# First score pass of an attention and mixture-of-experts block: two heads at a time in the two halves of the array

## The chip, the cores and the metric

The kernel runs on one core of one Trainium2 chip. Its time is the time on the device in microseconds, the median of several executions. Before the change three executions took 592.57 us in the median, 589.27 us at the least and 598.64 us at the most.

## The reference

The input is eight images ("image" here is one entry of the batch) of 512 tokens with 128 channels, in float32. For each of them

```python
h = _layernorm(x, axis=-1) * (1 + ca) + sa
x = x + ga * _L0_attn_ref(h, ...)
h = _layernorm(x, axis=-1) * (1 + cb) + sb
x = x + gb * _L0_ffn_ref(h, ...)
```

The six modulation rows (`sa`, `ca`, ...) come from a small product of a condition with `wmod`. The attention has 16 heads of 8 channels, is causal, and ends in a projection and a layer norm:

```python
att = jnp.einsum('bhtd,bhsd->bhts', q, k) * (1.0 / math.sqrt(Dh))
att = jnp.where(causal[None, None], att, -jnp.inf)
att = jax.nn.softmax(att, axis=-1)
o = jnp.einsum('bhts,bhsd->bhtd', att, v)
```

The feed-forward part has one shared expert of width 128 and eight routed experts of width 64, of which a token's two likeliest count; all eight are computed and multiplied by a coefficient that is zero for the others:

```python
shared_out = jnp.einsum('bsd,dh->bsh', shared_act * shared_up_out, shared_down)
expert_out = jnp.einsum('etd,edh->eth', jax.nn.silu(gate) * up, experts_down)
routed = jnp.einsum('eth,te->th', expert_out, coef)
```

## The kernel before

**Scores.** q and k are split into three bf16 parts each (`q_parts`, `k_parts`), written to DRAM and read back as stacks: for each head 72 rows (`KROWS`) hold all nine combinations of a part of q with a part of k, so that one bf16 product over 72 rows gives nearly exact scores. Scores are computed twice. The **first pass** (`s1`, L1003 to L1019) serves the row maximum alone: queries on the 128 partitions, `w` keys along the columns (128, 256, 384 or 512, by the block `qt` of queries), then a second product that adds the causal mask to the last 128 columns (L1017). VectorE reduces each bank to `row_max` (L844). A bank takes one head of 512 or 384 columns, two of 256, or four of 128, so a group of four heads takes 11 units (`S1_UNITS`); two banks alternate, and unit u waits until unit u - 2 is reduced. The maxima are split into three bf16 parts by two small VectorE operations (`msplit`, L853 and L855), transposed by TensorE (`max`, L1051), copied by ScalarE, and put by a DMA on the SP queue into three further rows of the stack of q. The **second pass** (`s2`, L1030) computes the scores transposed over 75 rows, with the maximum subtracted. ScalarE takes the exponential (L650), GpSimd cuts the triangle (L558), and `pv` (L1044) multiplies by the values, four heads at a time in four groups of 32 array columns.

**Banks.** There are eight PSUM banks: two for `s1`, two for `s2`, `pv_bank`, `misc`, `gate_bank`, `up_bank`. `misc` is shared by all small products in turn (`MISC_TASKS`): each waits until the one before it is read. The gate product (L1097) goes to `gate_bank` and the up product (L1108) to `up_bank`; VectorE multiplies the two (L922, L927). `up_bank` also holds the projection `y` (L1065, L1068), which ScalarE scales into `y_sb` (L683) and VectorE multiplies by gamma (L873).

**Order.** Each engine works through its queue in order. The order is written out by hand as tables: an image is four stages (`s` 0 to 3, one for each group of four heads) of 30 steps. `S1_STEPS`, `S2_STEPS` and `PV_STEPS` place the score and value units, `EXTRA` all other tasks. In stage s the first pass works on group s, the second on group s - 1, the values on s - 1 and s - 2. `LATER` shifts single tasks on VectorE, GpSimd or ScalarE by some steps. The feed-forward part of an image runs in the stages of the next one; the last image's runs alone at the end (`LAST`). `PROLOGUE` is what comes ahead of the first image.

**Queues.** The SP queue issues, in order, the writes of q and k parts (L438 to L443), the loads of the stacks (`load_stacks`, six a group, L422), and the DMA of the maxima (L456).

## Time and profile before

| what | value |
|---|---|
| median of 3 executions | 592.57 us (589.27 to 598.64) |
| profiled execution, its own time | 592.91 us |
| its span, first to last instruction | 591.2 us |
| mean granted TensorE clock | 0.916 |
| TensorE busy | 520.3 us, 88% |
| VectorE busy | 416.9 us, 71% |
| ScalarE busy | 299.3 us, 51% |
| GpSimd busy | 244.5 us, 41% |

The busy time of TensorE counts a matmul to its modelled end, and matmuls overlap, so the distance between two starts tells more of what one costs than its duration. Idle time of an engine counts only where another one waits for it. The granted clock is the share of the full 2.4 GHz that TensorE was given; it has two levels here, 1.0 and 0.5.

### The profile page before, as it was taken

What the parts mean: (1) busy time and instruction counts of PE and PEld (TensorE: products, weight loads), DVE (VectorE), ACT (ScalarE), POOL (GpSimd) and SP (SyncE); (2) the same over time, 40 slices, a digit from 0 to 9 for tenths busy, and PEclk for the clock granted to TensorE, in tenths of its full rate; (3) what the DMA queues carried; (4) which work ended last, traced back from release to release, by engine and by line L of the source; (5) the groups of instructions that cost most, each with busy time, mean ns of one, the idle gap of its engine ahead of it and who ended that gap; (6) DMA issues with size and microseconds to landing.
All of it is one profiled execution on the core that took longest, in us unless ns stands there. A gap on an engine that the chain in (4) does not pass through costs nothing.

```text
span 591.2 us, 10213 instructions
## 1 busy us (share of the span) xinstructions
PE 520.3 (88%) x3628; PEld 281.4 (48%) x3643; DVE 416.9 (71%) x877; ACT 299.3 (51%) x614; POOL 244.5 (41%) x299
## 2 busy tenths in 40 slices
PE   1647989899989999899989998999989998999567
PEld 1513434455644464456455554546445643645234
DVE  7458988687776868776878777686767677573045
ACT  1104546656565546655565647454655646455320
POOL 6024335713662257524572366235742424034210
PEclk9957899899997999899989999899979998599769
DMA  5171412321324113321332132412331121001000
GB/s 139 48 191 51 148 46 83 107 74 42 77 59 149 42 51 87 112 54 45 84 103 81 42 78 59 149 42 60 77 131 24 37 82 38 0 2 37 0 1 18
DMA packets 46930, 40.65 MB, mean 69 GB/s; under 512 B 8088, under 2 KB 42656, under 8 KB 46880
## 3 DMA queue, kind: packets, MB, share of 16 engines
q1 hardware_dynamic: 39232, 36.92, 22.1%
q10 hardware_dynamic: 7648, 3.09, 2.0%
q8 instruction: 29, 0.48, 0.4%
q14 instruction: 21, 0.17, 0.1%
HBM read 24.91 MB, written 14.68 MB: 67 GB/s over the span
## 4 chain that ended last, share of the span: by engine, by line
PE 72%; DVE 13%; ACT 6%; issue 4%; DMA 2%; SPq 1%; POOL 0%; DVEq 0%; POOLq 0%; ACTq 0%
PE pv_bank L1044 13%; PE s_bank L1015 11%; PE s_bank L1030 10%; DVE row_max L844 7%; PE gate_bank L1097 6%; PE gate_bank L1130 6%; PE up_bank L1108 6%; PE misc L973 5%; PE s_bank L1017 4%; PE misc L995 3%; ACT probs L650 3%; PE misc L1000 2%; PE up_bank L1068 2%; PE misc L1078 2%; ACT square L676 2%
## 5 line engine op out<-in xcount | busy, mean ns | idle before, releaser
L844 DVE TENSOR_REDUCE row_max<-s_bank 128x1 f32<-128x512 f32 (+3 forms) x352 | 213.0, 637 | 82.1 <-PE s_bank L1017 79.5
L650 ACT ACTIVATE probs<-s_bank 128x512 f32<-128x512 f32 x320 | 183.4, 598 | 105.9 <-PE s_bank L1030 103.4
L1015 PE MATMUL s_bank<-k_stack,q_stack 72*128 72x256 bf16 (+3 forms) x512 | 142.4, 319 | 17.2 <-DMA k_stack<-k_scr 8.3
L558 POOL TENSOR_SCALAR_AFFINE_SELECT probs<-probs 128x512 f32<-128x512 f32 (+1 forms) x96 | 80.2, 841 | 120.5 <-ACT probs L650 120.4
L1030 PE MATMUL s_bank<-q_stack,k_stack 75*128 75x128 bf16 (+3 forms) x512 | 118.7, 310 | 3.8 <-ACT probs L650 1.7
L1017 PE MATMUL s_bank<-causal,ident_bf 128*128 128x128 bf16 x512 | 103.8, 228 | 0.0
L1044 PE MATMUL pv_bank<-probs,v_aug 128*32 128x512 f32 (+3 forms) x1024 | 97.3, 485 | 0.0
L1015 PEld LDWEIGHTS s_bank<-k_stack,q_stack 72*128 72x128 bf16 x512 | 51.0, 100 | 81.1 <-DVE row_max L844 49.7
L1030 PEld LDWEIGHTS s_bank<-q_stack,k_stack 75*128 75x128 bf16 x512 | 42.0, 100 | 48.2 <-ACT probs L650 17.5
L1017 PEld LDWEIGHTS s_bank<-causal,ident_bf 128*128 128x128 bf16 x512 | 52.3, 102 | 24.3 <-issue 16.6
L543 POOL TENSOR_TENSOR hidden<-hidden,coef_sb 128x512 f32<-128x512 f32 x28 | 35.6, 1271 | 43.2 <-ACT coef_sb L696 43.0
L1097 PE MATMUL gate_bank<-h2T,wg 128*128 128x512 f32 x76 | 42.7, 644 | 0.1
L1108 PE MATMUL up_bank<-h2T,wu 128*128 128x512 f32 x76 | 41.1, 622 | 0.0
L1130 PE MATMUL gate_bank<-wd_b,hidden 128*128 128x128 f32 x280 | 37.2, 280 | 0.4
L1044 PEld LDWEIGHTS pv_bank<-probs,v_aug 128*32 128x32 f32 x1024 | 24.4, 114 | 27.5 <-issue 22.7
L1130 PEld LDWEIGHTS gate_bank<-wd_b,hidden 128*128 128x128 f32 x280 | 33.9, 191 | 2.4 <-issue 1.6
L864 DVE RECIPROCAL denom<-misc 128x16 f32<-128x16 f32 x32 | 8.1, 253 | 35.6 <-PE misc L973 35.6
L659 ACT ACTIVATE u_sb<-pv_bank 128x512 f32<-128x512 f32 x32 | 19.1, 597 | 25.1 <-PE pv_bank L1044 25.1
L922 DVE SCALAR_TENSOR_TENSOR silu_sb<-tanh_sb,gate_bank 128x512 f32<-128x512 f32 x38 | 25.9, 683 | 4.9 <-ACT tanh_sb L701 4.3
L701 ACT ACTIVATE tanh_sb<-gate_bank 128x512 f32<-128x512 f32 x38 | 22.7, 596 | 11.6 <-PE gate_bank L1097 11.6
L927 DVE SCALAR_TENSOR_TENSOR hidden<-silu_sb,up_bank 128x512 f32<-128x512 f32 x38 | 25.9, 680 | 3.4 <-PE up_bank L1108 3.4
L578 POOL TENSOR_SCALAR coef_parts<-coef 128x32 bf16<-128x32 f32 x8 | 2.4, 300 | 58.2 <-DVE coef L916 58.2
(150 smaller groups left out, 625.2 us busy)
## 6 DMA issues: line engine op xcount, KB each, us to landing
q_stack<-q_scr SPq DMA_DIRECT2D x96, 96.0 KB
k_stack<-k_scr SPq DMA_DIRECT2D x96, 96.0 KB
k_scr<-k_parts SPq DMA_DIRECT2D x14, 256.0 KB, 3.2
q_scr<-q_parts SPq DMA_DIRECT2D x7, 384.0 KB, 2.3
k_scr<-k_parts SPq DMA_DIRECT2D x7, 384.0 KB, 3.0
x_res<-in_L_attn_x SPq DMA_DIRECT2D x8, 256.0 KB, 3.4
out_x<-out_sb SPq DMA_DIRECT2D x8, 256.0 KB, 2.6
x_in<-in_L_attn_x ACTq DMA_DIRECT2D x7, 256.0 KB, 2.9
```

The costliest lines, as they stand in the source:

```text
L543: nc.gpsimd.tensor_tensor(hidden[:, a, :], hidden[:, a, :], coef_sb[:, :], ALU.mult).then_inc(weighted, 1)
L558: nc.gpsimd.affine_select(out=view, in_=view, compare_op=ALU.is_ge, fill=0.0, base=0, pattern=pat, channel_multiplier=-1).then_inc(probs_r ...
L650: nc.scalar.activation(dst, src, ACT.Exp, scale=SCALE).then_inc(exp_done, 1)
L844: nc.vector.reduce_max(row_max[s % 2][:, 0, h:h + nh, qt], s1_bank[u % 2][:, 0:nh * w].rearrange("p (h k) -> p h k", h=nh), AX_X).then_inc ...
L973: final = nc.tensor.transpose(dst[:, P * t:P * (t + 1)], src(t), idn[:, :])
L1015: nc.tensor.matmul(dst[:, w * i:w * (i + 1)], q_stack[0:KROWS, h, P * qt:P * (qt + 1)], k_stack[0:KROWS, h, 0:w], start=True, stop=False)
L1017: final = nc.tensor.matmul(dst[:, w * (i + 1) - P:w * (i + 1)], ident_bf[:, :], causal[:, :], start=False, stop=True)
L1030: final = nc.tensor.matmul(dst[:, at:at + w], k_stack[0:MROWS, hh, P * j:P * (j + 1)], q_stack[0:MROWS, hh, P * j:T], start=True, stop=True)
L1044: final = nc.tensor.matmul(pv_bank[VC * h:VC * (h + 1), P * j:T], v_aug[(it - (n < 0)) % 2][:, j, GH * g + h, :], probs[g % 2][:, h, P_AT[ ...
L1097: nc.tensor.matmul(gate_of(it, a)[:, :], wg[:, P * a:P * (a + 1)], h2T[:, :], start=True, stop=True).then_inc(gate_written, 1)
L1108: nc.tensor.matmul(up_of(it, a)[:, :], wu[:, P * a:P * (a + 1)], h2T[:, :], start=True, stop=True).then_inc(up_written, 1)
L1130: last_mm = nc.tensor.matmul(down_of(it)[:, P * t:P * (t + 1)], hidden[:, m, P * t:P * (t + 1)], wd_b[:, m, :], start=False, stop=(a == MB ...
```

## The change

The first pass takes two heads at a time. The first 64 of the 72 rows of a head are used. The even head's rows lie on partitions 0 to 63 (`q_stack`, `k_stack` as before), the odd head's on partitions 64 to 127 of two new tiles (`q_odd`, `k_odd`). The two products are built with a tile size of 64 by 128 at row 0 and at row 64, and write to two different banks. Their mask products follow, over all 128 rows. `S1_PAIRS` has six entries for a group, each of which fills two banks, so a group has 12 units. Three banks turn round; the third was `up_bank`. The up products of all images but the last one's go through `misc`, and `y` into `gate_bank`, where it is scaled and multiplied by gamma in place. `msplit` moves from VectorE to GpSimd. The stacks take 12 loads a group in place of six, and k is written in five parts. In the prologue x is loaded first, the copy `cond_rep` (`spread`) and the gate products come later. All tables of the order are new.

```diff
-S1_UNITS = ([(h, 1, 3) for h in range(GH)] + [(h, 1, 2) for h in range(GH)]
-            + [(0, 2, 1), (2, 2, 1)] + [(0, 4, 0)])
+S1_PAIRS = [((0,), 3), ((2,), 3), ((0,), 2), ((2,), 2), ((0, 2), 1), ((0, 2), 0)]
...
-S1_STEPS = [[0, 0, 7, 10, 12, 13, 14, 16, 16, 17, 21],
+S1_STEPS = [[0, 7, 12, 13, 14, 19],
...
-    "xin", "xs", "cond", "xn", "late", "xt", "gates0", "q", "gates1", "k", "gates2", "stack", "v", "gates3")]
+    "xin", "xs", "cond", "xn", "late", "xt", "q", "spread", "k", "stack", "v", "gates0", "gates1", "gates2", "gates3")]
...
+def hidden_made(eng, it, a, up_read, misc_read):
+    if it == B:
+        eng.wait_ge(up_read, a + 1)
+    elif it > 0:
+        eng.wait_ge(misc_read, misc_at(it, (s_of(it, "u", a), "u", a)) + 1)
...
-        s1_bank = [bank("s1_bank0"), bank("s1_bank1")]
+        s1_bank = [bank(f"s1_bank{i}") for i in range(3)]
...
-        Q_DMAS = 2 * PARTS
-        SCR_DMAS = 1 + 1 + 2 * (PARTS - 1)
+        Q_DMAS = 4 * PARTS
+        SCR_DMAS = PARTS + K_SLOTS
...
         def up_of(it, a):
-            return s1_bank[1] if last(it) and a % 2 else up_bank
+            return s1_bank[1 + a % 2] if last(it) else misc
...
+                for i, r in enumerate(ROTATIONS):
...
+                    for stack, odd, scr, at in ((q_stack, q_odd, q_scr, 0), (k_stack, k_odd, k_scr, DH * r)):
+                        sp.dma_start(stack[rows, heads, :],
+                                     scr[heads, at:at + SROWS, :].rearrange("h r t -> r h t")).then_inc(stacked[g], 16)
+                        sp.dma_start(odd[odd_rows, pair, :],
+                                     scr[GH * g + 1:GH * g + GH:2, at:at + DH * odd_parts, :]
+                                     .rearrange("h r t -> r h t")).then_inc(stacked[g], 16)
...
+                if name == "msplit":
+                    z = row_max[s % 2][:, :, :, :].rearrange("p k h t -> p k (h t)")
+                    n2 = it * (G * 2) + 2 * s
+                    pool.wait_ge(s1_reduced, it * (G * U1) + U1 * (s + 1))
+                    nc.gpsimd.tensor_tensor(z[:, 1, :], z[:, 0, :], upper(z[:, 0, :]), ALU.subtract).then_inc(max_step, 1)
+                    pool.wait_ge(max_step, n2 + 1)
+                    nc.gpsimd.tensor_tensor(z[:, 2, :], z[:, 1, :], upper(z[:, 1, :]), ALU.subtract).then_inc(max_step, 1)
...
+                    for odd in range(2):
+                        u = U1 * s + 2 * a + odd
+                        h = heads[0] + odd
+                        dve.wait_ge(s1_written, it * (G * U1) + (u + 1))
+                        nc.vector.reduce_max(row_max[s % 2][:, 0, h:h + 2 * nh - 1:2, qt],
+                                             s1_bank[u % 3][:, 0:nh * w].rearrange("p (h k) -> p h k", h=nh),
+                                             AX_X).then_inc(s1_reduced, 1)
...
                     need(pe, s1_reduced, it * (G * U1) + (u - 1))
                     w = P * (qt + 1)
-                    dst = s1_bank[u % 2]
-                    for i in range(nh):
-                        h = GH * s + h0 + i
-                        nc.tensor.matmul(dst[:, w * i:w * (i + 1)], q_stack[0:KROWS, h, P * qt:P * (qt + 1)],
-                                         k_stack[0:KROWS, h, 0:w], start=True, stop=False)
-                        final = nc.tensor.matmul(dst[:, w * (i + 1) - P:w * (i + 1)], ident_bf[:, :], causal[:, :],
-                                                start=False, stop=True)
-                    final.then_inc(s1_written, 1)
+                    even, odd = s1_bank[u % 3], s1_bank[(u + 1) % 3]
+                    for i, h in enumerate(heads):
...
+                        nc.tensor.matmul(even[:, cols], q_stack[0:HALF, hh, queries], k_stack[0:HALF, hh, 0:w],
+                                         start=True, stop=False)
+                        nc.tensor.matmul(odd[:, cols], q_odd[HALF:P, hh // 2, queries], k_odd[HALF:P, hh // 2, 0:w],
+                                         start=True, stop=False)
+                        for dst in (even, odd):
+                            final = nc.tensor.matmul(dst[:, w * (i + 1) - P:w * (i + 1)], ident_bf[:, :], causal[:, :],
+                                                    start=False, stop=True)
+                            if i == len(heads) - 1:
+                                final.then_inc(s1_written, 1)
...
                 if name == "u":
-                    if a == 0:
-                        pe.wait_ge(y_scaled, it)
                     if not last(it):
-                        need(pe, up_read, it * MB + (a - MB))
+                        take_misc(it, (s, "u", a))
```

**TensorE, stage 1 of a steady image**, up to the transpose of the maxima (`max`). Before:

```order
L1015 MATMUL s_bank<-k_stack,q_stack 128x128
L1017 MATMUL s_bank<-causal,ident_bf 128x128
L1030 MATMUL s_bank<-q_stack,k_stack 128x128
L1030 MATMUL s_bank<-q_stack,k_stack 128x384
L1030 MATMUL s_bank<-q_stack,k_stack 128x256 x2
L1051 MATMUL misc<-ident_bf,row_max 48x128
L1030 MATMUL s_bank<-q_stack,k_stack 128x256 x2
L1044 MATMUL pv_bank<-probs,v_aug 32x512 x4
L1000 MATMUL misc<-wv,h1T 128x128 x4
```

With the change (L1051 is the even head's product, L1053 the odd's, L1056 the mask, L1070 the second pass, L1084 the values, L1091 the transpose):

```order
L1051 MATMUL s_bank<-k_stack,q_stack 128x128
L1053 MATMUL s_bank<-k_odd,q_odd 128x128
L1056 MATMUL s_bank<-causal,ident_bf 128x128 x2
L1070 MATMUL s_bank<-q_stack,k_stack 128x128
L1070 MATMUL s_bank<-q_stack,k_stack 128x384
L1070 MATMUL s_bank<-q_stack,k_stack 128x256 x4
L1084 MATMUL pv_bank<-probs,v_aug 32x512 x4
L1091 MATMUL misc<-ident_bf,row_max 48x128
L1051 MATMUL s_bank<-k_stack,q_stack 128x512
```

Two products of the second pass and the value product have moved to the front of the transpose, and the two heads' products stand side by side.

**TensorE, stage 2**, where the products of the feed-forward part stand (L1137 is a gate product, L1146 an up product, L1007 a transpose). With the change:

```order
L1146 MATMUL misc<-h2T,wu 128x512
L1137 MATMUL gate_bank<-h2T,wg 128x512
L1007 MATMUL misc<-ident,u_sb 128x128 x4
L1070 MATMUL s_bank<-q_stack,k_stack 128x128
L1070 MATMUL s_bank<-q_stack,k_stack 128x384
...
L1070 MATMUL s_bank<-q_stack,k_stack 128x256 x4
L1146 MATMUL misc<-h2T,wu 128x512
L1137 MATMUL gate_bank<-h2T,wg 128x512
L1007 MATMUL misc<-ident_bf,coef_parts 128x128 x4
L1084 MATMUL pv_bank<-probs,v_aug 32x512 x4
```

Before, the same products stand so:

```order
L973 MATMUL misc<-ident,u_sb 128x128 x4
L1030 MATMUL s_bank<-q_stack,k_stack 128x256 x2
L1108 MATMUL up_bank<-h2T,wu 128x512
...
L1044 MATMUL pv_bank<-probs,v_aug 32x512 x4
L1097 MATMUL gate_bank<-h2T,wg 128x512
L973 MATMUL misc<-ident_bf,coef_parts 128x128 x4
L1108 MATMUL up_bank<-h2T,wu 128x512
L1051 MATMUL misc<-ident_bf,row_max 48x128
```

The up products now write `misc`, as the transposes around them do, and each of these waits until the one before it is read.

**The SP queue, first image**, between the first loads and the maxima. Before there are six loads like these for a group; with the change a group has twelve:

```order
L422 DMA k_stack<-k_scr 24x4x512
L438 DMA q_scr<-q_parts 96x1536
L440 DMA k_scr<-k_parts 96x1536
L442 DMA k_scr<-k_parts 96x1024
L443 DMA k_scr<-k_parts 96x512
L442 DMA k_scr<-k_parts 96x512
L443 DMA k_scr<-k_parts 96x1024
L422 DMA q_stack<-q_scr 24x4x512
L422 DMA k_stack<-k_scr 24x4x512
```

```order
L439 DMA k_odd<-k_scr 16x2x512
L459 DMA q_scr<-q_parts 12x8x512 x3
L462 DMA k_scr<-k_parts 12x8x512 x5
L437 DMA q_stack<-q_scr 24x4x512
L439 DMA q_odd<-q_scr 24x2x512
L437 DMA k_stack<-k_scr 24x4x512
L439 DMA k_odd<-k_scr 24x2x512
L437 DMA q_stack<-q_scr 24x4x512
L439 DMA q_odd<-q_scr 24x2x512
```

The writes of q and k have become eight (three and five), and loads of `q_odd` and `k_odd` stand between those of the stacks.

## Rows read from the trace of the kernel before

**Rows 1.** The page, parts 1 and 4: busy time by engine, and the chain.

```profile
PE 520.3 (88%) x3628; PEld 281.4 (48%) x3643; DVE 416.9 (71%) x877; ACT 299.3 (51%) x614; POOL 244.5 (41%) x299
...
PE 72%; DVE 13%; ACT 6%; issue 4%; DMA 2%; SPq 1%; POOL 0%; DVEq 0%; POOLq 0%; ACTq 0%
```

**Rows 2.** Span and mean granted TensorE clock.

```profile
core 0: 591.2 us, clock 0.916
```

**Rows 3.** Groups by shape, PE: count, busy us, mean ns, idle before by releaser.

```profile
L1015 PE MATMUL s_bank<-k_stack,q_stack 72*128 72x512 bf16 x128 | 50.9, 425 | 10.7 <-DMA k_stack<-k_scr 8.3 <-DVE row_max L844 2.1
...
L1051 PE MATMUL misc<-ident_bf,row_max 128*48 128x128 bf16 x32 | 7.5, 233 | 15.2 <-issue 13.2 <-ACT h1T L623 1.0 <-DVE row_max L855 0.9
```

**Rows 4.** Waits: who for whom, us in total, times, longest.

```profile
PEld s_bank L1015 <- DVE row_max L844: 49.7, 133, 3.0
```

**Rows 5.** Timeline, PE, first-pass products of 512 columns: start us, us.

```profile
250.08 0.38 PE L1015 MATMUL s_bank<-k_stack,q_stack 72*128 72x512 bf16 x1
250.30 0.22 PE L1017 MATMUL s_bank<-causal,ident_bf 128*128 128x128 bf16 x1
```

**Rows 6.** Timeline, products of 128 columns, then the value products.

```profile
258.91 0.22 PE L1015 MATMUL s_bank<-k_stack,q_stack 72*128 72x128 bf16 x1
258.92 0.10 PEld L1017 LDWEIGHTS s_bank<-causal,ident_bf 128*128 128x128 bf16 x1
258.97 0.22 PE L1017 MATMUL s_bank<-causal,ident_bf 128*128 128x128 bf16 x1
...
259.21 0.22 PE L1017 MATMUL s_bank<-causal,ident_bf 128*128 128x128 bf16 x1
...
259.36 0.64 PE L1044 MATMUL pv_bank<-probs,v_aug 128*32 128x512 f32 x4
```

**Rows 7.** Timeline, PE, 256 columns, and the product with one row.

```profile
272.14 0.27 PE L1015 MATMUL s_bank<-k_stack,q_stack 72*128 72x256 bf16 x1
272.25 0.22 PE L1017 MATMUL s_bank<-causal,ident_bf 128*128 128x128 bf16 x1
...
272.79 0.38 PE L1124 MATMUL gate_bank<-zero_row 1*128 1x512 bf16 x1
273.11 0.38 PE L1130 MATMUL gate_bank<-wd_b,hidden 128*128 128x128 f32 x1
```

**Rows 8.** Timeline before the transpose of the maxima in stage 1.

```profile
240.49 0.39 PE L1030 MATMUL s_bank<-q_stack,k_stack 75*128 75x256 bf16 x2
...
240.91 1.26 POOL L571 TENSOR_TENSOR x_res<-x_res,beta_a 128x512 f32<-128x512 f32 x1
241.02 1.18 DVE L855 TENSOR_TENSOR row_max<-row_max 128x16 f32<-128x16 f32 x1
...
242.30 0.27 PE L1051 MATMUL misc<-ident_bf,row_max 128*48 128x128 bf16 x1 [1.42 <-issue]
```

**Rows 9.** Windows: length, busy of five engines, clock, DMA share, GB/s.

```profile
218.00:281.10 63.10, 60.29 (x450) 32.75 (x450) 48.30 (x104) 37.38 (x77) 30.82 (x36) 0.97 0.27 77
344.50:409.10 64.60, 61.79 (x450) 33.45 (x450) 48.30 (x104) 37.38 (x77) 30.82 (x36) 0.95 0.26 75
242.20:245.60 3.40, 3.30 (x14) 1.14 (x15) 3.23 (x9) 1.28 (x3) 2.13 (x2) 0.50 0.29 109
34.40:88.00 53.60, 43.36 (x278) 20.04 (x279) 46.77 (x87) 21.81 (x40) 20.59 (x20) 0.78 0.35 99
```

**Rows 10.** Groups by shape, DVE.

```profile
L927 DVE SCALAR_TENSOR_TENSOR hidden<-silu_sb,up_bank 128x512 f32<-128x512 f32 x38 | 25.9, 680 | 3.4 <-PE up_bank L1108 3.4
```

**Rows 11.** Groups by shape, POOL.

```profile
L580 POOL TENSOR_TENSOR coef_rest<-coef,coef_parts 128x32 f32<-128x32 f32 x8 | 2.0, 245 | 0.7
```

**Rows 12.** Timeline of the first image, SP queue and first product.

```profile
31.41 0.35 SPq L438 DMA_DIRECT2D q_scr<-q_parts  x1
...
34.38 0.59 PE L1015 MATMUL s_bank<-k_stack,q_stack 72*128 72x512 bf16 x1 [8.30 <-DMA k_stack<-k_scr]
...
37.35 0.31 SPq L422 DMA_DIRECT2D q_stack<-q_scr  x1
```

180 lines of the change are left out of this document (95 added, 85 removed), and 27 rows, old and new, of tables (LATER, S1_STEPS, S2_STEPS).

## The prediction, made before the changed kernel was run

> **What bounds the kernel now.** I first read the busy times and the chain of the page [rows 1]: TensorE is busy 88% of the span and has 72% of the chain, VectorE 71% and 13%. So TensorE's stream of products is the bound in most of the span, and the question is what else stands in it. The granted clock is 0.916 in the mean [rows 2]. The windows [rows 9] say where the rest lies. In two steady images TensorE is busy 60.29 of 63.10 us and 61.79 of 64.60 us with the same 450 products. In the first image it is busy only 43.36 of 53.60 us, beside a VectorE that is busy 46.77 us: there VectorE's reductions bound, and TensorE has 10 us to spare.
>
> The groups and waits [rows 3, 4] show what TensorE waits for: 15.2 us ahead of the 32 transposes of the maxima, and 2.1 us on VectorE ahead of the widest first-pass products. Their weight loads waited 49.7 us, 133 times, but weights are loaded ahead, so this is mostly no loss of products. The timeline [rows 8] shows the worst wait ahead of a transpose: its products end near 240.9, VectorE's second `msplit` operation takes 1.18 us beside a GpSimd operation of 1.26 us, and the transpose starts at 242.30 after 1.42 us of idle time. The clock then is 0.50 for the next 3.40 us [rows 9]. The two steady images differ in length by 1.5 us, with clocks of 0.97 and 0.95.
>
> **The change, step by step.** Distances between starts at full clock are 0.22 us for 512 columns, 0.11 for 256 and 0.06 for 128 [rows 5 to 7]; 384 lies between, 0.17.
>
> *Columns saved.* A pair streams once where two heads streamed one after the other. That is 0.22 + 0.17 + 0.11 + 0.06 = 0.56 us for each of 64 pairs of heads, 35.8 us at full clock, 39.1 at the mean of 0.916. That the two do run side by side is not in this trace for row halves. The nearest row is the value product: four products in four column groups last 0.64 us together [rows 6]. I take full overlap, less 0.01 us a pair (256 pairs, 2.6 us). The bounds are that and no saving at all.
>
> *Pauses between modes.* The two products use the array in another mode than the mask products behind them. Where the trace changes mode it shows a pause. From a mask product to the value product it is 259.36 - 259.21 = 0.15 us in place of 0.06 [rows 6]; out of the product with one row, 512 columns take 273.11 - 272.79 = 0.32 us in place of 0.22 [rows 5, 7]. So 0.09 to 0.10 us a change, 0.095 taken. Neighbours that differ in mode number 238 in the order before and 746 in the new one: 508 more, 48.3 us. No row shows a change between modes that both use all 128 columns and at least 64 rows, so the lower bound is nothing, the upper 48.3 us.
>
> The Trainium skill ("TensorEngine Tiling (Array Packing)", Key Properties) says that any change of the tiling mode, not of the tile, drains TensorE; by it the full 48.3 us stand, without it the kernel would be 48.3 us faster than my sum.
>
> *Net stream:* 48.3 + 2.6 - 39.1 = +11.8 us, +12. In the first image 64 of the changes (6 us) fall into TensorE's spare 10 us [rows 9]: -5.
>
> *Weight loads.* They last 0.10 us (258.92), yet the products stand 0.06 us apart [rows 6], all on the same rows of the array. So loads are hidden already and the halves hide nothing more: 0. The Trainium skill ("TensorE: Matmul & The Clock Gate", Part 3, The mechanism) says that a load overlaps a running product only if their row groups differ. The trace here disagrees: by the rule 256 odd heads' loads of 0.10 us, 25.6 us, would go too; by the row nothing.
>
> *`msplit` on GpSimd.* It leaves VectorE, and with it the collision of [rows 8]. GpSimd's nearest operation, of twice the width, takes 245 ns [rows 11]; two take 0.5 us. What queues behind them on GpSimd is the selection of the next triangle, which the value product needs only a stage later. The cover has grown as well: in stage 1 two more second-pass products (0.22 us) and a value product (about 0.5 us) stand ahead of the transpose. I take 60% of the 15.2 us [rows 3]: -9. Bounds 0 and -15.
>
> *Third bank.* A pair waits for the first half of the pair before, so TensorE may run one and a half units ahead instead of one. The visible waits are small: -3.5 in the steady images, bounds 0 and -8. The cost of 32 more reductions lies on VectorE, which loses `msplit` and is not the bound in steady images: 0.
>
> *Clock.* In each of six images a stretch at half clock stands behind the wait of [rows 8]. It costs 1.5 us per 3.4 us, by the two images of [rows 9] (clock 0.97 against 0.95). Four images have a clock of 0.95 like the second (about 6.8 us, 3.0 us lost), two 0.97 (1.5 lost): 15 us to be had if the wait is gone. But the pauses leave TensorE without products more often elsewhere. I take -10, bounds -15 and +11.
>
> *Up products through `misc`.* 35 of the 40 now hold it until VectorE has multiplied, 680 ns [rows 10] behind a busy queue. In stage 2 the transposes of `u_sb` are queued behind one up and one gate product, about 1.7 us of cover; VectorE has to go through the routing's small operations first. Behind this transpose stand the second-pass products and all of ScalarE's exponentials. I take 1 us an image, +7; bounds 0 and 35 x 0.68 = 24. `y` in the gate bank: the first gate product comes a stage later, 0.
>
> *SP queue and prologue.* Six writes and their landing took from 31.41 to 37.35, 5.9 us; now eight, +2 us ahead of the second group. A DMA takes the queue 0.31 to 0.35 us at the least to issue [rows 12], so six more loads are +2 us ahead of the first products, which started at 34.38, less about 1 for a k that is ready earlier. The second group's loads and the maxima behind them are late too. +3, bounds -2 and +8. Later stages have over 30 us between load and use: 0.
>
> **Sum.** Profiled execution 592.9 + 12 - 5 - 9 - 3.5 - 10 + 7 + 3 = 587.4, so 587 us. The profiled execution is 0.3 us above the median of 592.6, so no correction. A change of under 2% (580.7 to 604.4) can't be told from none.
>
> **Rivals.**
>
> *All waits and half-clock stretches gone.* The pauses don't bring the clock down, and the hand-offs through `misc` are covered: 587 - 5 - 7 = 575. For it: the collision is gone for certain, and the order now places work ahead of the transpose. Against: VectorE still has four halves of first-pass work in a row before the end of stage 1.
>
> *No pause in the new mode.* 587 - 48 + 5 = 544. For it: no row shows this mode. Against: both kinds of change that rows do show pause alike.
>
> *Slower: the clock.* Pauses of 0.19 us a pair are densest where the 128 and 256 columns stand: a pair of 128 columns has 0.18 us of products and 0.19 of pause. With the waits around, such a place may do what 1.42 us of idle did. The old stretches stay (+10), and each of seven images gets another of 3.4 us (7 x 1.5 = +10.5): 608. It decides from about twelve stretches of 3.4 us on beyond those of the forecast (17.4 us to the bound of 604.4, 1.5 each). For it: TensorE's pauses grow from 23 to 71 us. Against: each pause is a tenth of a microsecond, and the wait of [rows 8] is fourteen times as long.
>
> *The pair doesn't overlap,* so the change doesn't do what it says: the odd product waits for the even one. 587 + 39 = 626. Against: the column groups overlap.
>
> **Chances.** Forecast 0.42 (its own range 580 to 598), everything gone 0.24, no pause 0.08, the clock 0.18, no overlap 0.05, the rest (a late queue, a longer hold of `misc`, 600 to 615) 0.03. The range of 8 in 10 takes in the forecast, the 575 with 8 us below it and the 608 with 2 above it: 567 to 610. It leaves out 544 and 626. Faster by over 2%: 0.24 + 0.08 + 0.02 of the forecast's lower end = 0.34. Slower: 0.18 + 0.05 + 0.02 = 0.25. Within: 0.41.
>
> **What would show it.** Starts of even and odd products 0.01 us apart prove the overlap, 0.2 us refute it. From the start of a 512-column pair to its mask product 0.31 us show the pause, 0.22 us refute it. Idle time ahead of the transposes should fall to about 6 us, that ahead of TensorE's transposes of `u_sb` grow by up to 7. A steady image should have a clock of 0.97 or more and last 63 to 64 us; 66 us with 0.93 would be the slower rival. The first product of the first pass should start at 35 to 37 us. My forecast is wrong above all if the clock goes either way, since that one term can weigh 25 us.

## The result: 2.2% slower

The changed kernel takes 605.48 us (median of 4 runs, 604.77 to 606.85) against 593.93 (4 runs, 589.27 to 598.64) of the kernel before: a ratio of 1.0224, interval [1.0155, 1.0293]. So it is slower beyond the interval, though not for certain by over 2%. Ratios here and below are of the fast executions alone and medians of all, and the kernel before has slow ones as well (up to 8 in 19, 594 to 599 us at a lower clock), so a ratio can stand some tenths of a per cent above that of the medians. The profiled execution took 605.75 us. The forecast was 587 with a range of 567 to 610, so the time lies inside the range and on the other side of no change.

The page's parts 1 and 4 and the clock, which answer to [rows 1, 2]:

```profile
PE 520.3 (86%) x3628; PEld 251.1 (42%) x3643; DVE 379.7 (63%) x845; ACT 295.4 (49%) x614; POOL 256.0 (42%) x363
...
PE 75%; DVE 10%; ACT 5%; SPq 3%; DMA 3%; issue 2%; ACTq 1%; POOL 1%; POOLq 0%; DVEq 0%
...
core 0: 604.0 us, clock 0.938
```

TensorE is as long busy as before, although 256 products no longer stream by themselves. VectorE lost 37 us of work and 3% of the chain. The clock is better than before, and the kernel is slower all the same.

Windows (length, busy of five engines, clock, DMA share, GB/s) of before, first the six images between the first and the last. Then of the changed kernel: its first image, the six, and one of them. The other windows of before are in [rows 9].

```profile
88.00:473.90 385.90, 368.26 (x2690) 200.37 (x2701) 289.76 (x625) 224.21 (x462) 183.26 (x216) 0.96 0.26 75
```

```profile
36.10:99.50 63.40, 48.99 (x280) 18.67 (x280) 43.23 (x83) 21.30 (x40) 22.95 (x28) 0.63 0.33 98
99.50:489.80 390.30, 365.94 (x2691) 176.61 (x2702) 261.10 (x601) 221.35 (x462) 191.13 (x263) 1.00 0.28 82
230.50:295.30 64.80, 60.75 (x450) 29.40 (x452) 43.51 (x100) 36.89 (x77) 32.12 (x44) 1.00 0.28 83
```

Of the 12.8 us between the spans, 1.7 lie ahead of the first product (36.1 against 34.4), 9.8 in the first image (63.4 against 53.6, clock 0.63 against 0.78) and 4.4 in the six images, where the clock is now 1.00 but for the first (66.1 us at 0.98). The last image and the tail gave 3 back.

Groups by shape on TensorE, answering to [rows 3]:

```profile
L1070 PE MATMUL s_bank<-q_stack,k_stack 75*128 75x512 bf16 x128 | 48.5, 395 | 7.7 <-DMA q_stack<-max_rows 3.9 <-ACT probs L677 3.8
L1051 PE MATMUL s_bank<-k_stack,q_stack 64*128 64x512 bf16 x64 | 26.2, 409 | 8.1 <-DMA k_odd<-k_scr 6.3 <-DVE row_max L876 1.7
L1051 PE MATMUL s_bank<-k_stack,q_stack 64*128 64x384 bf16 x64 | 22.1, 346 | 6.6 <-DVE row_max L876 6.6
L1051 PE MATMUL s_bank<-k_stack,q_stack 64*128 64x256 bf16 x64 | 18.4, 288 | 6.1 <-DVE row_max L876 6.0
L1051 PE MATMUL s_bank<-k_stack,q_stack 64*128 64x128 bf16 x64 | 14.8, 232 | 3.7 <-DVE row_max L876 3.7
L1070 PE MATMUL s_bank<-q_stack,k_stack 75*128 75x256 bf16 x128 | 23.4, 286 | 4.4 <-ACT probs L677 3.8
L1146 PE MATMUL misc<-h2T,wu 128*128 128x512 f32 x70 | 37.2, 612 | 3.4 <-DVE logit L913 3.4
L1091 PE MATMUL misc<-ident_bf,row_max 128*48 128x128 bf16 x32 | 7.4, 232 | 2.9 <-issue 1.5 <-POOL row_max L586 1.3
```

The same groups of before that aren't in [rows 3] (first pass of 384, 256 and 128 columns, second pass of 512 and 256, up products):

```profile
L1015 PE MATMUL s_bank<-k_stack,q_stack 72*128 72x384 bf16 x128 | 43.8, 343 | 4.9 <-DVE row_max L844 4.3
L1015 PE MATMUL s_bank<-k_stack,q_stack 72*128 72x256 bf16 x128 | 29.3, 281 | 0.1
L1015 PE MATMUL s_bank<-k_stack,q_stack 72*128 72x128 bf16 x128 | 19.1, 226 | 1.6 <-DVE row_max L844 1.4
L1030 PE MATMUL s_bank<-q_stack,k_stack 75*128 75x512 bf16 x128 | 45.9, 391 | 2.0 <-ACT probs L650 1.2 <-DMA q_stack<-max_rows 0.8
L1030 PE MATMUL s_bank<-q_stack,k_stack 75*128 75x256 bf16 x128 | 26.2, 293 | 0.8 <-ACT probs L650 0.2
L1108 PE MATMUL up_bank<-h2T,wu 128*128 128x512 f32 x76 | 41.1, 622 | 0.0
```

The 12.3 us that went from ahead of the transposes (15.2 to 2.9) are back elsewhere, in the first image and in the six. First-pass products of 384 to 128 columns wait 16.4 us (before 6.6), second-pass products of 512 and 256 columns 12.1 (before 2.8), up products 3.4 (before 0). In the six images alone TensorE's idle time, the length of the window less the busy time, grew from 17.6 to 24.4 us.

Timelines of the changed kernel (start us, us): a pair of 128 columns, then one of 384, each with its mask products.

```profile
253.82 0.23 PE L1051 MATMUL s_bank<-k_stack,q_stack 64*128 64x128 bf16 x1
253.82 0.23 PE L1053 MATMUL s_bank<-k_odd,q_odd 64*128 64x128 bf16 x1
...
253.98 0.29 PE L1056 MATMUL s_bank<-causal,ident_bf 128*128 128x128 bf16 x2
```

```profile
247.12 0.33 PE L1051 MATMUL s_bank<-k_stack,q_stack 64*128 64x384 bf16 x1
247.13 0.33 PE L1053 MATMUL s_bank<-k_odd,q_odd 64*128 64x384 bf16 x1
247.39 0.29 PE L1056 MATMUL s_bank<-causal,ident_bf 128*128 128x128 bf16 x2
```

The two heads start 0.01 us apart or less: they run side by side. From the pair to its first mask product it is 0.16 us at 128 columns, in place of 0.06, and 0.27 at 384, in place of 0.17. So the pause on leaving this mode is 0.10 us at either width, as between the modes of [rows 5 to 7]. A pair of 128 columns saves 0.06 us and pays two pauses. Counted over the whole trace, neighbours that differ in mode are 746 (before 238), as the forecast had counted them.

### The profile page after: what moved, and what is told of

The parts are those of the page before. It is cut to its first block, busy times and chain, and to the rows that moved or that the text cites. A ratio compares the mean times of both kernels' runs of the same rounds, so it can differ in the third digit from the quotient of the medians.

```text
span 604.0 us, 10440 instructions
## 1 busy us (share of the span) xinstructions
PE 520.3 (86%) x3628; PEld 251.1 (42%) x3643; DVE 379.7 (63%) x845; ACT 295.4 (49%) x614; POOL 256.0 (42%) x363
## 4 chain that ended last, share of the span: by engine, by line
PE 75%; DVE 10%; ACT 5%; SPq 3%; DMA 3%; issue 2%; ACTq 1%; POOL 1%; POOLq 0%; DVEq 0%
PE pv_bank L1084 14%; PE s_bank L1070 10%; PE s_bank L1051 10%; PE s_bank L1056 8%; PE gate_bank L1137 6%; PE gate_bank L1168 6%; PE misc L1146 5%; DVE row_max L876 5%; PE misc L1007 5%; PE misc L1029 3%; ACT probs L677 3%; PE gate_bank L1108 2%; PE misc L1034 1%; DVE x_n L827 1%; PE misc L1091 1%
## 5 line engine op out<-in xcount | busy, mean ns | idle before, releaser
L876 DVE TENSOR_REDUCE row_max<-s_bank 128x1 f32<-128x384 f32 (+3 forms) x384 | 212.5, 595 | 89.0 <-PE s_bank L1056 86.8
L677 ACT ACTIVATE probs<-s_bank 128x512 f32<-128x512 f32 x320 | 181.5, 594 | 139.4 <-PE s_bank L1070 136.8
L1070 PE MATMUL s_bank<-q_stack,k_stack 75*128 75x128 bf16 (+3 forms) x512 | 116.8, 310 | 13.5 <-ACT probs L677 8.7
L577 POOL TENSOR_SCALAR_AFFINE_SELECT probs<-probs 128x512 f32<-128x512 f32 (+1 forms) x96 | 76.8, 800 | 110.3 <-ACT probs L677 110.2
L1051 PE MATMUL s_bank<-k_stack,q_stack 64*128 64x512 bf16 (+3 forms) x256 | 81.6, 319 | 24.5 <-DVE row_max L876 18.1
L1084 PE MATMUL pv_bank<-probs,v_aug 128*32 128x512 f32 (+3 forms) x1024 | 96.4, 465 | 0.3 <-POOL probs L577 0.3
L1053 PE MATMUL s_bank<-k_odd,q_odd 64*128 64x512 bf16 (+3 forms) x256 | 81.6, 319 | 0.0
L1056 PE MATMUL s_bank<-causal,ident_bf 128*128 128x128 bf16 x512 | 75.5, 231 | 0.0
L1070 PEld LDWEIGHTS s_bank<-q_stack,k_stack 75*128 75x128 bf16 x512 | 43.5, 101 | 60.0 <-ACT probs L677 33.6
L1051 PEld LDWEIGHTS s_bank<-k_stack,q_stack 64*128 64x128 bf16 x256 | 23.8, 93 | 86.9 <-DVE row_max L876 49.9
L1056 PEld LDWEIGHTS s_bank<-causal,ident_bf 128*128 128x128 bf16 x512 | 29.5, 98 | 40.5 <-issue 28.9
L1137 PE MATMUL gate_bank<-h2T,wg 128*128 128x512 f32 x76 | 41.0, 621 | 1.1 <-issue 1.1
L1146 PE MATMUL misc<-h2T,wu 128*128 128x512 f32 x70 | 37.2, 612 | 3.4 <-DVE logit L913 3.4
L1084 PEld LDWEIGHTS pv_bank<-probs,v_aug 128*32 128x32 f32 x1024 | 22.8, 111 | 34.0 <-issue 27.4
L953 DVE SCALAR_TENSOR_TENSOR silu_sb<-tanh_sb,gate_bank 128x512 f32<-128x512 f32 x38 | 26.1, 686 | 14.1 <-ACT tanh_sb L727 14.1
L727 ACT ACTIVATE tanh_sb<-gate_bank 128x512 f32<-128x512 f32 x38 | 22.7, 596 | 22.4 <-PE gate_bank L1137 22.4
L961 DVE SCALAR_TENSOR_TENSOR hidden<-silu_sb,misc 128x512 f32<-128x512 f32 x35 | 24.1, 688 | 14.7 <-PE misc L1146 12.7
```

The source lines that it names most:

```text
L577: nc.gpsimd.affine_select(out=view, in_=view, compare_op=ALU.is_ge, fill=0.0, base=0, pattern=pat, channel_multiplier=-1).then_inc(probs_r ...
L677: nc.scalar.activation(dst, src, ACT.Exp, scale=SCALE).then_inc(exp_done, 1)
L876: nc.vector.reduce_max(row_max[s % 2][:, 0, h:h + 2 * nh - 1:2, qt], s1_bank[u % 3][:, 0:nh * w].rearrange("p (h k) -> p h k", h=nh), AX_X ...
L1051: nc.tensor.matmul(even[:, cols], q_stack[0:HALF, hh, queries], k_stack[0:HALF, hh, 0:w], start=True, stop=False)
L1053: nc.tensor.matmul(odd[:, cols], q_odd[HALF:P, hh // 2, queries], k_odd[HALF:P, hh // 2, 0:w], start=True, stop=False)
L1056: final = nc.tensor.matmul(dst[:, w * (i + 1) - P:w * (i + 1)], ident_bf[:, :], causal[:, :], start=False, stop=True)
```

## The experiments

The forecast's sum had five places where it could fail: pairs, queue, third bank, shared bank, and the gain from waits and clock. The first runs take the change apart; the later ones build on the kernel before. Ratios are to runs of before on the same chip (medians 593.3 to 593.8, where not given otherwise). A difference between two runs by their ratios can come out some us apart from that of their medians; where it matters both are given.

### The pauses: masks behind both pairs

```diff
-                                         start=True, stop=False)
+                                         start=(i == 0), stop=False)
...
+                    for i, h in enumerate(heads):
...
-                                                    start=False, stop=True)
+                                                    start=False, stop=(i == len(heads) - 1))
```

> The changed kernel, but in units with two pairs of heads (256 and 128 columns) all four products of the 64-row mode come first and the four mask products after them. That is two changes of mode fewer in each of 64 units, 128 fewer. Theory A (each change of mode costs TensorE 0.095 to 0.10 us, and in steady images nothing hides it): 12 to 13 us less than the changed kernel's 605.5, so 593 us, and less only by what falls into waits in the first image, 591 to 597. Rival B (the pauses lie in TensorE's waits for VectorE, and the loss comes from the new waits and hand-offs): within 2 us of 605.5.

Measured: 593.85 us, ratio 1.0073 [1.0040, 1.0105]. A hit: 11.6 us for 128 changes of mode (two in each of the 64 units that hold two pairs, those of 256 and 128 columns). Its first image and its six:

```profile
36.50:98.20 61.70, 44.77 (x278) 17.27 (x278) 43.61 (x83) 21.28 (x40) 22.64 (x28) 0.70 0.34 99
98.20:479.20 381.00, 358.35 (x2703) 171.98 (x2702) 261.01 (x601) 220.83 (x462) 190.75 (x264) 1.00 0.29 84
```

The six images took 9.3 us less than in the change at the same clock. The six images hold 96 of the 128 changes, so the pauses are on the path in steady images, and at 0.10 us each they weigh what the forecast gave them.

### No pairs, and no second queue entries

```diff
-  nc.tensor.matmul(even[:, cols], q_stack[0:HALF, hh, queries], k_stack[0:HALF, hh, 0:w],
+  nc.tensor.matmul(even[:, cols], q_stack[0:KROWS, hh, queries], k_stack[0:KROWS, hh, 0:w],
...
-  nc.tensor.matmul(odd[:, cols], q_odd[HALF:P, hh // 2, queries], k_odd[HALF:P, hh // 2, 0:w],
+  nc.tensor.matmul(odd[:, cols], q_stack[0:KROWS, hh + 1, queries], k_stack[0:KROWS, hh + 1, 0:w],
```

> The changed kernel with its order, banks and loads, but both products of a pair are taken over 72 rows of the full stacks, so they run one after the other in the mode of the mask products. 512 changes of mode are gone, and the columns are streamed twice. Theory A: -49 us of pauses, +36 to +39 us of columns, so 592 to 596 us. Rival C (the pairing pays and something else lost the time): 605.5 + 36 us or nearly, 630 to 642. Both heads' products should start 0.22 us apart at 512 columns in place of 0.01.

Measured: 595.95 us, 1.0116 [1.0033, 1.0199]. A hit. The pairs cost 9.5 us net in this kernel (6.4 by the ratios). Not 512 changes of mode went, as the expectation says: counted in the trace, neighbours that differ in mode are 273 in place of 746, so 473 went. Some pairs stand beside a product of yet another mode, where a pause stays without them. The other 35 above the 238 of before belong to the new order.

The second run takes out the loads of `k_odd` and `q_odd` as well (the `sp.dma_start(odd[...])` of the change; four entries of the queue per pair of parts become two).

> As e2, and the loads of the odd heads' stacks, which nothing reads now, are left out: six loads a group. Theory D (the longer SP queue costs time in the first image alone): the first product starts 2 us earlier, TensorE's 3.1 us wait for the maxima's DMA goes, and the kernel is 3 to 6 us faster than e2. Rival: the queue is hidden by other waits of the first image, within 1.5 us of e2.

Measured: 593.63 us, 1.0024 [0.9985, 1.0062]; 2.3 us for the queue by the medians (5.4 by the ratios), so between the 3 to 6 of theory D and the 1.5 of its rival. TensorE's wait for the DMA of the maxima went as expected (2.9 to 0.9 us ahead of the second pass), but the first product starts 1.0 us earlier, not 2. Windows of the two, first image and six:

```profile
36.20:99.40 63.20, 50.06 (x278) 24.07 (x279) 43.24 (x83) 21.30 (x40) 22.97 (x28) 0.64 0.33 97
99.40:483.60 384.20, 361.84 (x2702) 194.27 (x2700) 260.91 (x601) 220.65 (x462) 190.84 (x263) 1.00 0.29 83
```

```profile
35.20:95.20 60.00, 46.54 (x279) 22.36 (x280) 43.62 (x83) 21.29 (x40) 22.14 (x28) 0.70 0.31 78
95.20:478.30 383.10, 360.69 (x2703) 194.03 (x2701) 260.90 (x601) 220.65 (x462) 191.68 (x264) 1.00 0.26 67
```

The first image without pairs is 63.2 us, with pairs 63.4: the pauses and the saved columns together make no difference there. The six images are 384.2 against 390.3, 1.0 us an image. The queue shows at the start (first product 35.2 against 36.2) and in the first image (60.0 against 63.2).

### Pairs only where they are wide

```diff
+                        if qt == 3:
...
+                        else:
+                            for dst, j in ((even, hh), (odd, hh + 1)):
+                                nc.tensor.matmul(dst[:, cols], q_stack[0:KROWS, j, queries], k_stack[0:KROWS, j, 0:w],
+                                                 start=True, stop=False)
```

> The changed kernel, with pairs in the 64-row mode only where they have 512 columns; the narrower ones are taken over 72 rows one after the other, as in e2. Against the changed kernel 384 changes of mode go (-38 us) and 0.67 us of columns a group come back (+21 us). Theory A: 605.5 - 17 = 588.5, or from e2 596 - 1.3 = 594.7, so 588 to 595 us, and under e2, since at 512 columns a pair saves 0.22 us and pays 0.20. Rival C (pairing is worth its price at all widths): above e2's 596.

Measured: 593.25 us, 1.0052 [1.0015, 1.0089]. A hit, and 12.2 us under the change. Against the run with no pairs at all (595.95) it is 2.7 us less (3.8 by the ratios). There 64 pairs of 512 columns save 64 x 0.22 = 14.1 us of columns, and by the trace they bring 89 changes of mode (362 against 273), 8.9 us. At 512 columns a pair gains a little. The narrower ones, each with masks of its own, pay more than they save; with the masks behind both pairs (593.85, above) pairs of all widths do as well as this run.

### The third bank and the shared bank

Both without pairs and with half the loads. The first run gives the up products their own bank again and leaves the first pass two; the second keeps the up products in `misc`, with two banks for the first pass, so the last two lines of this diff are the first run's alone. In both, the even head's products and masks now come ahead of the odd head's, and each head waits for its own bank alone.

```diff
-        s1_bank = [bank(f"s1_bank{i}") for i in range(3)]
+        s1_bank = [bank(f"s1_bank{i}") for i in range(2)]
...
-        pv_bank, misc, gate_bank = (bank(x) for x in ("pv_bank", "misc", "gate_bank"))
+        pv_bank, misc, gate_bank, up_bank = (bank(x) for x in ("pv_bank", "misc", "gate_bank", "up_bank"))
...
-                        take_misc(it, (s, "u", a))
+                        need(pe, up_read, (it - 1) * MB + a)
```

> e3 (unpaired, six loads a group), with the up products in a bank of their own again and two banks for the first pass, each first-pass unit waiting for its own bank. Theory H (the up products' hand-offs through the shared bank cost about 1 us an image): 5 to 7 us under e3, 586 to 589 us. Rival I (the third bank was worth as much as the hand-offs cost): within 2 us of e3's 593.6, or above it.

> The kernel with no pairs and no second queue entry for K, whose up products write the shared bank (as in the change), but whose first score pass has two banks as before (the third stands idle). It parts the 9.2 us by which the run with an own bank for the up products and two score banks beat the run with the shared bank and three. Theory L (the third score bank is worth little, 0 to 2 us, and the hand-offs of the shared bank cost 9 to 11): 593 to 596 us. Rival M (the third bank is even a loss, since it lets first products run ahead and heap up work on VectorE, and the hand-offs cost about 5): 588 to 591 us. Rival N (the third bank is worth 4 or more, as the forecast had it): 597 us or more.

Measured: 584.41 us, 0.9914 [0.9866, 0.9962], and 593.17 us, 1.0021 [0.9961, 1.0081]. The first went the expected way and further (9.2 us under the run with half the loads, 5 to 7 expected). The second says whose the 9.2 are: the hand-offs of `misc` cost 8.8 (593.17 - 584.41; 6.3 by the ratios), and the third bank, with the order of products that goes with it, is worth nothing (593.63 with it, 593.17 without). The six images of the one and the other, and the first up product of one steady image in the second:

```profile
92.20:469.10 376.90, 361.61 (x2702) 193.46 (x2700) 259.12 (x601) 220.61 (x462) 191.19 (x264) 1.00 0.26 68
```

```profile
95.60:480.30 384.70, 365.24 (x2691) 192.73 (x2701) 260.39 (x601) 220.58 (x462) 190.42 (x263) 0.99 0.26 67
...
261.88 1.12 PE L1139 MATMUL misc<-h2T,wu 128*128 128x512 f32 x2 [0.49 <-DVE logit L910]
```

The up product waits until VectorE's routing has read the router's product out of `misc`, 0.49 us an image (3.4 us in all). That is under half of the 8.8. The rest is spread over shorter waits and, in the first image and the start of the second, over half clock.

### The split of the maxima on GpSimd, in the kernel before

```diff
-    "pool": {(0, "s2", 9): 8, (1, "k", 0): 4, (1, "ot", 0): 4, (1, "s2", 7): 4, (2, "s2", 3): 4, (2, "s2", 9): 1,
+    "pool": {(0, "msplit", 0): 4, (1, "msplit", 0): 12, (2, "msplit", 0): 8,
+        (0, "s2", 9): 8, (1, "k", 0): 4, (1, "ot", 0): -2, (1, "s2", 7): 4, (2, "s2", 3): 4, (2, "s2", 9): 1,
...
-                    nc.vector.tensor_tensor(z[:, 1, :], z[:, 0, :], upper(z[:, 0, :]), ALU.subtract)
+                    nc.gpsimd.tensor_tensor(z[:, 1, :], z[:, 0, :], upper(z[:, 0, :]), ALU.subtract)
```

> The kernel before with one part of the change alone: msplit on GpSimd in place of VectorE, at the same steps, and the addition to x_res ahead of the statistics of y as in the changed kernel. Theory E (the collision of the second msplit operation with GpSimd makes the 1.42 us wait, and that wait brings the clock down in six images): the wait falls by 0.7 us or more, the stretches at half clock behind it go, 0.7 x 7 + up to 15 us less: 575 to 585 us. Rival: GpSimd is itself late there (rstd of y ends at the same moment), and 0.7 us of wait still brings the clock down: 588 to 593.

Measured: 584.22 us, 0.9871 [0.9781, 0.9960]. A hit. The timeline where [rows 8] stand, the clock in the window of [rows 9], and the group of the transposes:

```profile
241.40 0.21 POOL L566 TENSOR_TENSOR row_max<-row_max 128x16 f32<-128x16 f32 x1
...
241.69 0.21 POOL L568 TENSOR_TENSOR row_max<-row_max 128x16 f32<-128x16 f32 x1
...
242.00 0.22 PE L1051 MATMUL misc<-ident_bf,row_max 128*48 128x128 bf16 x1 [0.63 <-issue]
```

```profile
242.20:245.60 3.40, 3.40 (x31) 1.61 (x30) 2.74 (x11) 2.16 (x6) 1.60 (x2) 1.00 0.17 61
...
L1051 PE MATMUL misc<-ident_bf,row_max 128*48 128x128 bf16 x32 | 7.2, 224 | 22.7 <-issue 18.1 <-POOL row_max L568 4.6
```

The wait in stage 1 fell from 1.42 to 0.63 us and the half clock behind it is gone, in five of the six images; in one it still stands, from 178.9 to 182.3 us. But the waits ahead of all 32 transposes grew, from 15.2 to 22.7 us: the kernel is 9 us faster (8 by the ratio) with more idle time there. What was gained was the clock, not the length of that wait. The next run starts the maxima of stage 1 one step later (`24: [("max", "cur")]` in place of 23).

> e4, and the transpose of the maxima of stage 1 one step later, behind two more second-pass products of 256 columns, as in the changed kernel. Theory E (idle time ahead of that transpose is what lengthens a steady image and brings the clock down): the wait falls by another 0.2 us an image and no steady image has a stretch at half clock: 1 to 4 us under e4, 580 to 583 us. Rival: in e4 the wait is already short enough, within 1 us of e4.

Measured: 580.24 us, 0.9844 [0.9776, 0.9912]. The number lies in the expected range, but not for the reason given. The six images of the run before this one and of this one:

```profile
92.00:467.10 375.10, 355.49 (x2702) 195.39 (x2700) 256.34 (x577) 223.07 (x462) 191.79 (x264) 1.00 0.27 77
```

```profile
91.70:467.30 375.60, 354.83 (x2703) 194.67 (x2702) 256.18 (x577) 223.05 (x462) 192.12 (x264) 1.00 0.27 77
```

The one stretch at half clock that was left is gone, as theory E had it, but the six images are no shorter. The profiled executions differ mainly behind them (114.2 and 110.8 us), so that the later step gives anything in steady images isn't shown. What is left stands in stage 3. There, on GpSimd and then TensorE:

```profile
273.79 1.28 POOL L545 TENSOR_TENSOR hidden<-hidden,coef_sb 128x512 f32<-128x512 f32 x1
275.02 0.64 POOL L560 TENSOR_SCALAR_AFFINE_SELECT probs<-probs 128x512 f32<-128x512 f32 x1
275.63 0.21 POOL L567 TENSOR_TENSOR row_max<-row_max 128x16 f32<-128x16 f32 x1
...
276.24 0.22 PE L1052 MATMUL misc<-ident_bf,row_max 128*48 128x128 bf16 x1 [1.33 <-issue]
```

VectorE's last maximum had started at 272.41 and lasted 0.69 us. From 273.1 the split waited in GpSimd's queue, behind 1.92 us of other work. The wait of 1.33 us stands in each of the six images, in the run before as in this one, and no half clock follows it. So the next run has stage 3's split back on VectorE (`if name == "msplit" and s == 3`), and one more adds the changed kernel's order ahead of the first image.

> The kernel before with the negation and split of the maxima on GpSimd in stages 0 to 2 only (in stage 3, the fourth, on VectorE as before) and the first score block's maximum at step 24. Theory J (GpSimd's own work of stage 3, the state's and the gate's, now stands behind the split, which lengthened that stage from 18.4 to 19.5 us an image in the run that moved the split alone; back on VectorE it costs its old wait of about 0.4 us and gives 1.1 us back, seven images): 573 to 577 us, under the 580.2 of the run with all four stages on GpSimd. Rival K (stage 3 is longer because it now receives work that stage 1 had, 18.4 to 15.6 us, so nothing comes back): 579 to 584 us.

> The run of the split on GpSimd outside stage 3, with the order of the changed kernel's first products as well: the x products first, the spreading of q and k between them, the gate products last. Theory: the first pair's K rows are ready about 1 us earlier and the gate products fall in image 0's idle, 1 to 3 us under that run. Rival: image 0 is bound by VectorE's and ScalarE's copies, the same time within 1 us, or up to 2 us more if the q products are late.

Measured: 573.57 us, 0.9637 [0.9582, 0.9692], and 573.37 us, 0.9646 [0.9588, 0.9704]. The first hits theory J: 6.7 us, of which the profile shows 6.0 in the six images (375.6 to 369.6). The prologue is worth nothing by itself, as its rival said. The first run's stage 3 and its six images:

```profile
208.03 1.10 POOL L560 TENSOR_SCALAR_AFFINE_SELECT probs<-probs 128x1024 f32<-128x1024 f32 x1 [0.70 <-ACT probs L660]
208.49 0.66 DVE L862 TENSOR_TENSOR row_max<-row_max 128x16 f32<-128x16 f32 x1
209.15 1.28 POOL L545 TENSOR_TENSOR hidden<-hidden,coef_sb 128x512 f32<-128x512 f32 x1
209.19 1.27 DVE L864 TENSOR_TENSOR row_max<-row_max 128x16 f32<-128x16 f32 x1
...
210.56 0.22 PE L1060 MATMUL misc<-ident_bf,row_max 128*48 128x128 bf16 x1 [0.29 <-issue]
```

```profile
90.50:460.10 369.60, 354.20 (x2691) 194.70 (x2702) 267.88 (x589) 222.94 (x462) 190.33 (x252) 1.00 0.27 78
```

On VectorE the two operations take 1.93 us beside two of GpSimd, each ending within 0.03 us of its neighbour there, and TensorE still waits only 0.29 us, since they start at once. These are the two fastest versions of all, 3.6% under the kernel before.

### The same return of stage 3, in the changed kernel

> The changed kernel with one edit: in stage 3 the negation and split of the maxima are on VectorE (step 26 of its list, behind the last maximum), in stages 0 to 2 on GpSimd as in the change. In the kernel before, the same return of stage 3 gave 6.7 us (580.2 to 573.6, stage 3 from 19.5 to 18.4 us an image). Theory J (the place of the split in stage 3 costs the change the same): 597 to 600 us, and stage 3 of a steady image from 20.1 to about 19 us. Rival P (in the changed kernel stage 3 is held by the up products in the shared bank and by the pauses, GpSimd has slack there): 603 to 607 us. Rival Q (at step 26 VectorE has another operation ahead of the split and the split comes later than on GpSimd): 607 us or more.

Measured: 609.52 us, 1.0320 [1.0240, 1.0399] (before: 592.92). Theory J fell. The time lies in the range of rival Q, but its reason isn't seen: the split comes no later. In the changed kernel GpSimd and VectorE in stage 3 stand like this:

```profile
289.19 1.28 POOL L562 TENSOR_TENSOR hidden<-hidden,coef_sb 128x512 f32<-128x512 f32 x1 [0.47 <-ACT coef_sb L722]
290.50 0.22 POOL L584 TENSOR_TENSOR row_max<-row_max 128x16 f32<-128x16 f32 x1
```

```profile
289.66 0.76 DVE L876 TENSOR_REDUCE row_max<-s_bank 128x2 f32<-128x256 f32 x2 [1.75 <-PE s_bank L1056]
```

The last maximum ends at 290.42 and the split starts at 290.50, and so in every image: it never waited here, so nothing could come back. With the split on VectorE it starts 0.04 us behind the last maximum in steady images, and the transpose stands 1.3 to 1.4 us behind the start of the split in either run, with no wait ahead of it. The run's six images (391.3 us) are as long as the change's (390.3). Its tail is longer, 58.6 against 56.4 us, at a clock of 0.77 against 0.82. The interval overlaps that of the change; why it came out 4 us above is open.

### More products in the first image

The products of the first head pair are made three times in stages 0 and 1 of image 0 (the repeats write the same scores again).

```diff
+                        for _ in range(2 if it == 0 and s < 2 and i == 0 else 0):
+                            nc.tensor.matmul(even[:, cols], q_stack[0:HALF, hh, queries], k_stack[0:HALF, hh, 0:w],
+                                             start=True, stop=True)
+                            nc.tensor.matmul(odd[:, cols], q_odd[HALF:P, hh // 2, queries], k_odd[HALF:P, hh // 2, 0:w],
+                                             start=True, stop=True)
```

> The changed kernel; in the first two stages of the first image each first-pass pair of products at the first head of a unit is computed three times (the first two results are overwritten), which gives TensorE about 6 us more of products at half clock, in a stretch where it waits 13 us for VectorE and DMAs. Theory F (the first image lost 9.8 us because idle time kept the clock at half from 34 to 75 us): the granted clock of the first two stages rises, and the kernel is no slower in spite of the extra products, 600 to 605 us. Rival G (the waits themselves, for reductions and the late DMA of the maxima, are the loss, and the clock is only their companion): clock unchanged or no help, 606 to 611 us.

Measured: 605.18 us, 1.0267 [1.0195, 1.0339]. The window from the first product to the end of the first stretch at half clock, and the rest of image 0; below it the like windows of the change:

```profile
36.40:57.20 20.80, 16.34 (x81) 5.54 (x82) 13.80 (x28) 1.74 (x3) 5.99 (x9) 0.50 0.44 131
57.20:99.30 42.10, 35.08 (x248) 13.55 (x247) 29.48 (x56) 19.67 (x37) 16.64 (x20) 0.80 0.28 82
```

```profile
36.10:75.20 39.10, 28.04 (x127) 10.35 (x127) 28.35 (x53) 8.11 (x15) 15.90 (x17) 0.50 0.42 122
75.20:99.50 24.30, 20.95 (x155) 8.32 (x153) 14.88 (x30) 13.19 (x25) 7.05 (x11) 0.85 0.19 60
```

With the added products the first stretch at half clock ends 18 us earlier, at 57.2 in place of 75.2, as theory F had it. The first image is 62.9 us long in place of 63.4, and the time of the kernel is the same (605.18 and 605.48). So 48 more products neither cost nor gave a measurable time. How much the better clock gave and how much the added work took isn't separated, and the run doesn't decide between the two expectations.

## Why the prediction was wrong, step by step

| term | forecast | by medians | by ratios, of 591 | from |
|---|---|---|---|---|
| pairs: columns, pauses, first image | +12 - 5 = +7 | +9.5 | +6 | change less the run without pairs |
| queue and prologue (measured: the loads alone) | +3 | +2.3 | +5 | without pairs, less half the loads |
| third bank | -3.5 | +0.5 | 0 | three banks less two, up products in `misc` |
| up products in `misc` | +7 | +8.8 | +6 | `misc` less own bank |
| split on GpSimd, clock | -9 - 10 = -19 | -8.9 | -5 | own bank, two banks, no pairs, less before (593.3) |
| sum | -5.5 | +12.2 | +13 | |

A single difference is uncertain by some 2 to 6 us (the intervals of the ratios reach 0.3 to 0.9% to either side); the 10 us or more by which the last term missed are more than that. The differences of ratios are turned into us with 591 us for the kernel before. The last term also holds what the new order and the new prologue cost or gave.

**The step that failed is the gain, -9, -3.5 and -10.** The forecast took 60% of the idle time ahead of the transposes of the maxima [rows 3] as time to be had. That idle time went, more than was forecast (15.2 to 2.9 us), and hardly any time came with it: the products of both score passes wait longer by 19 us, by their rows for VectorE's maxima, ScalarE's exponentials and the DMA of the maxima. Part of that stands with the three banks (below). The run with own banks, which has neither pairs nor a third bank nor up products in `misc`, shows the rest: ahead of the transposes 3.4 us are left, but TensorE's idle time in the six images fell only from 17.6 to 15.3 us, 2.3 in all.

The size of the clock was right or too small. In the kernel before with the split alone moved the six images came down by 10.8 us (385.9 to 375.1) with 2.0 us more idle time (19.6), so 12.8 us of busy time went with the half clock. In the run with own banks all half clock in the six images went as well (0.96 to 1.00), but they came down by 9.0 only, 6.7 of it busy time (368.3 to 361.6). So the new order gave back about 6 us as time in which TensorE is busy, not as waits: at the same clock the kernel before with the split moved is busy 355.5 us with the same products. Some 3 of the 6 would be changes of mode, 210 in the six images in place of 180, at 0.10 us each; where the others lie isn't known. The first image also paid for the split: moved alone, it took that image from 53.6 to 58.1 us. The kernel before with the split moved and stage 3 left out has 369.6 us in its six images: some 20 us were to be had (593.3 to 573.6), though not in the changed order. Of the 7.3 us between 376.9 and 369.6 all is busy time (361.6 and 354.2). Which of the changed tables costs it wasn't tried.

**Third bank.** With three banks the first-pass products of 384 to 128 columns wait more for the maxima, not less (17.9 us by their groups, with two banks 9.3), and the time is the same. The forecast's -3.5 rested on waits [rows 3, 4] that a bank more doesn't take away. That VectorE sets the pace there, whatever the number of banks, is argued, not shown.

**Pairs.** The mechanism held at each step: side by side, 0.10 us a pause, nothing from weight loads. The size was off twice, in opposite directions. The saved columns were taken at the mean clock of 0.916, but the steady images ran at full clock, where the forecast's own figures make +15.1 (48.3 + 2.6 - 35.8). And of its 508 changes of mode 35 came with the new order and not with the pairs; with 473 it is +11.7, 1.5 an image. Measured are 1.0 in each of six, as if a third of that fell into waits that stood there anyway. In the first image pairs cost 0.2, where the forecast, with its pauses hidden and its saved columns counted, makes 1.5 - 5 = -3.5: there the columns gave nothing either. The rest of the 9.5 lies in the last image and the tail (114.2 against 110.4 us behind the six), and there it isn't shown to be the pairs' work: the run with half the loads, without pairs too, has 114.3.

By the rule of the Trainium skill ("TensorEngine Tiling (Array Packing)", Key Properties) any change of the tiling mode drains TensorE. The trace agrees: 0.10 us on leaving the 64-row mode, and 11.6 us less with 128 changes fewer, 0.09 each.

The rule of "TensorE: Matmul & The Clock Gate" (the Trainium skill, Part 3, The mechanism) on loads in other rows would have given 25.6 us. With the pairs put back the time rose by 9.5; no such gain shows.

**Shared bank.** +7 was nearly right in size (8.8) and wrong in place. The transposes of `u_sb` did not wait longer; the up products themselves waited for the router's values to be read.

**The rivals.** The slower rival named 608 and the time came near it, but for another reason: its mark was a steady image of 66 us at a clock of 0.93, and there it is 64.8 at 1.00. The clock did fall in the first image (0.78 to 0.63), without the pairs too (0.64). Half the loads bring it to 0.70, and an own bank for the up products leaves it there; why it isn't back at 0.78 is open. Neither "everything gone" nor "no pause" nor "no overlap" happened. None of the rivals was the one that came: idle time that moves to another product, a new order that gives back part of what the clock brought, and the hand-offs and pauses paid nearly in full.

## What to carry to other kernels

Idle time ahead of one instruction is no saving until the trace shows that what is queued behind it would not wait for the same producer; what stands with a wait, half clock behind it, can be worth more than its length. Two heads side by side in 64 rows each pay up to two changes of mode a pair, so put all pairs of a unit together and the products of the other mode behind them, and pair narrow products only so. When an operation moves to another engine, ask for each stage what stands ahead of it in the new queue: in the kernel before it was right in three stages of four and leaving out the fourth was worth 6.7 us, in the changed kernel nothing stood ahead of it in any.

## What the runs showed of the hardware

- Leaving the mode of two products with 64 rows costs 0.10 us, the same at 128 and 384 columns, though all columns and rows are in use on both sides; their starts lie 0.00 to 0.01 us apart.
- The negation and split of a 128x16 tile takes two operations of 0.21 us each on GpSimd. On VectorE they took 0.17 us each in stage 3 of the changed kernel with the split returned (at 290.94), but 0.66 and 1.27 us beside GpSimd operations of 1.10 and 1.28 us, and ended within 0.03 us of these (208.03 to 209.19 above).
- In six steady images of the kernel before, a wait of 1.42 us was followed by half clock; with 0.63 us in the same place it came in one image of six and for 3.4 us, and the kernel was 8 to 9 us faster. The length of the wait alone doesn't tell: ahead of the transpose in stage 3 the same run waits 1.33 us in each of the six, and no half clock follows.
